# Transfers cut at partition 112, and a last stage with spread inverse roots and an affine step on GpSimd, in a two-layer graph network

## What is computed

```python
h = x @ w_in + b_in
Wij = (ssp(f_ij @ w_f1 + b_f1) @ w_f2 + b_f2) * rcut_ij[:, None]
agg = segment_sum(h[idx_j] * Wij, idx_i)
x1 = layernorm(x + ssp(agg @ w_o1 + b_o1) @ w_o2 + b_o2)

dinv = rsqrt(deg)                       # degree with the self loop
out = segment_sum((x1 @ W)[src] * (dinv[src] * dinv[dst])[:, None], dst) + b
out = relu((out - mean) * rsqrt(var + 1e-5) * gamma + beta)   # over the nodes
result = layernorm(x1 + out)                                  # over the 128 features
```

## Time and profile before

| | |
|---|---|
| runs shown | 7341.11, 7344.63, 7347.38 us, median 7344.63 us |
| the profiled execution | 7344.54 us, its span 7342.8 us |
| mean granted TensorE clock | 0.779 |
| busy share: PE, PE weight load, DVE, ACT, POOL | 79%, 56%, 72%, 48%, 69% |
| instructions | 156,129 |
| DMA | 695.39 MB, mean 95 GB/s |

### The profile page before, as it was taken

The page is one execution under the profiler, slowest core; times in us unless marked ns, Lnnn a source line. Parts: engine busy times, 40 slices in busy tenths (PEclk is TensorE's granted clock), DMA queues, the critical chain, the costliest instruction groups (busy, mean ns, idle before and its releaser), DMA issues. The chain is left out here.

```text
span 7342.8 us, 156129 instructions
## 1 busy us (share of the span) xinstructions
PE 5812.5 (79%) x41800; PEld 4127.1 (56%) x41800; DVE 5317.5 (72%) x14198; ACT 3558.1 (48%) x5657; POOL 5086.9 (69%) x5375
## 2 busy tenths in 40 slices
PE   7778787877788777777777765676999999999994
PEld 6555555555556555555555544554666666666662
DVE  7777777777778888888888873456777777777765
ACT  2555555555555555555555550063333333333334
POOL 4577777777777777777777774435777777777770
PEclk6565666666656888887777776677999999999995
DMA  4222222221223444443333327724222222222222
GB/s 129 80 85 85 86 86 72 57 57 56 57 57 99 119 118 119 122 115 98 96 98 99 97 75 234 240 95 141 77 75 77 77 76 76 76 77 76 76 77 73
DMA packets 512129, 695.39 MB, mean 95 GB/s; under 512 B 255298, under 2 KB 367644, under 8 KB 510878
## 3 DMA queue, kind: packets, MB, share of 16 engines
q1 hardware_dynamic: 317008, 347.69, 16.9%
q0 software_dynamic: 181376, 321.40, 14.9%
q10 hardware_dynamic: 13498, 24.07, 1.0%
HBM read 450.80 MB, written 241.85 MB: 94 GB/s over the span
## 5 line engine op out<-in xcount | busy, mean ns | idle before, releaser
L1694 POOL DMA_INDIRECT msg_tab<-big x3224 | 3159.3, 980 | 1065.3 <-issue 1041.2
L2245 POOL DMA_INDIRECT big<-y_parts,big x1616 | 1590.1, 984 | 551.5 <-issue 487.1
L2326 ACT CAST big<-ps 128x980 bf16<-128x980 f32 x804 | 783.9, 975 | 1277.8 <-PE ps L2274 1276.8
L2286 PE MATMUL ps<-big 128*128 128x384 bf16 x6566 | 1199.4, 326 | 0.2 <-ACT big L2326 0.2
L2378 DVE TENSOR_SCALAR big<-big,dstF 128x343 bf16<-128x343 f16 (+2 forms) x3216 | 985.3, 338 | 235.7 <-PE ps L2274 129.5
L1383 ACT CAST big<-ps 128x512 bf16<-128x512 f32 x403 | 236.0, 586 | 1511.2 <-DMA msg_tab<-big 1507.4
L2286 PEld LDWEIGHTS ps<-big 128*128 128x128 bf16 x6566 | 581.7, 97 | 350.0 <-issue 3.9
L1178 PE MATMUL ps<-big 2*128 2x512 bf16 x806 | 336.3, 509 | 547.6 <-ACT big L1367 547.4
L1186 PE MATMUL ps<-big 128*128 128x128 f32 x3224 | 706.5, 390 | 10.9 <-ACT big L1378 7.2
L1186 PEld LDWEIGHTS ps<-big 128*128 128x128 f32 x3224 | 635.4, 293 | 20.2 <-ACT big L1378 20.0
L1491 DVE TENSOR_REDUCE big<-big 128x8 f32<-128x784 f32 x403 | 629.9, 1563 | 0.0
(11 more groups left out here) (289 smaller groups left out, 10746.0 us busy)
## 6 DMA issues: line engine op xcount, KB each, us to landing
arena<-msg_tab SPq DMA_DIRECT2D x97, 727.5 KB, 4.4
big<-msg_tab SPq DMA_DIRECT2D x97, 630.5 KB
big<-in_edge_attr SPq DMA_DIRECT2D x403, 128.0 KB
msg_tab<-big POOLq DMA_INDIRECT x3224
big<-msg_tab SPq DMA_DIRECT2D x97, 388.0 KB
msg_tab<-big SPq DMA_DIRECT2D x97, 291.0 KB
big<-y_parts,big POOLq DMA_INDIRECT x1616
big<-h_parts SPq DMA_DIRECT2D x403, 48.0 KB
```

Source lines behind the costliest of these rows:

```text
L1694: nc.gpsimd.indirect_dma_start(out=m.msg_tab[:, :], out_offset=bass.IndirectOffsetOnAxis(ap=sidx[s][:, j:j + 1], axis=0), in_=row[s][:, j, ...
L2245: nc.gpsimd.indirect_dma_start(out=m.grow[s][:, 3 * D * j:3 * D * j + 3 * D], out_offset=None, in_=m.y_parts[:, :], in_offset=bass.Indirec ...
L2286: mm = pe.matmul(ps_rows, m.cnt[h][:, a, :], m.y_part[:, HALF * h + a, :], start=(h == 0 and a == 0), stop=(h == 1 and a == HALF - 1))
L2326: nc.scalar.copy(m.cnt[h][:, :, SLOTS * i:SLOTS * i + SLOTS].rearrange("p h (a w) -> p h a w", a=2), ps_cnt[i % 2][:, :, 0:SIDE * HALF].re ...
```

## The change

`node_update`: every transfer between DRAM and a tile of 125 partitions is issued as two, over partitions 0 to 111 and 112 to 124 (`PIECES`): the loads of the degrees and of `agg`, and the stores of dinv, `x1_tab`, `y_parts` and `y_tab`. The semaphores count 32 in place of 16 for a block.

`norm_and_store` is written anew. The inverse roots are read from DRAM into all 128 partitions by six transfers (`SPREAD`, of 2, 3, 5, 5, 5 and 5 blocks), before x1 on SP's queue. DVE multiplies 15 of the 25 blocks by them and POOL the other 10 (blocks 1 and 3 of each five). PE has no product there. The affine step of part C is on POOL, without the relu; the relu is folded into DVE's residual step as a maximum with 0, with the product still in PSUM. DVE's steps are interleaved so that none waits for the one just before it. There are four output buffers. The table load of ACT comes right behind the square root. The output stores and x1's loads are split at 112 partitions. All loops of the stage are written out.

```diff
+PIECES = ((0, WIDE), (WIDE, NP))
+XN = 4
+SPREAD = ((0, 2), (2, 5), (5, 10), (10, 15), (15, 20), (20, 25))
+X1_LOADS = 5
...
             def load(q, s):
-                sp.dma_start(agg[s], m.agg_sum[0:N, :].rearrange("(p c) d -> p (c d)", p=NP)[:, bass.ds(q * (B * F), B * F)]
-                             ).then_inc(tabs_in[s], 16)
+                for a, z in PIECES:
+                    sp.dma_start(agg[s][a:z, :],
+                                 m.agg_sum[0:N, :].rearrange("(p c) d -> p (c d)", p=NP)[a:z, bass.ds(q * (B * F), B * F)]
+                                 ).then_inc(tabs_in[s], 16)
...
-                    dve.wait_ge(x1_stored[s], 16 * turn + 16)
+                    dve.wait_ge(x1_stored[s], 32 * turn + 32)
...
         @block.sync
         def _(sp):
-            def load(q, s, turn):
-                sp.wait_ge(spread, free(q))
-                sp.dma_start(drow[s], m.dinv_tab[bass.ds(q * BW, BW)].rearrange("(o n) -> o n", o=1)).then_inc(row_in[s], 16)
-            over(sp, NB, load)
+            for k, (a, z) in enumerate(SPREAD):
+                sp.dma_start(dinv_bc[:, a * BW:z * BW],
+                             m.dinv_tab[a * BW:z * BW].rearrange("(o n) -> o n", o=1).to_broadcast([P, (z - a) * BW])
+                             ).then_inc(dinv_in[k], 16)
+            x1_rows = m.x1_tab.rearrange("(p c) d -> p (c d)", p=NP)
+            n = NC * D // X1_LOADS
+            for k in range(X1_LOADS):
+                for a, z in PIECES:
+                    sp.dma_start(x1[a:z, k * n:k * n + n], x1_rows[a:z, k * n:k * n + n]).then_inc(x1_in[k], 16)
...
+        @block.gpsimd
+        def _(pool):
+            for q in turns:
...
+                nc.gpsimd.tensor_tensor(part(q), part(q), scales(q), ALU.mult).then_inc(pool_scaled, 1)
+            pool.wait_ge(bn_ready, 4)
+            for q in range(NB):
+                if q > 1:
+                    pool.wait_ge(turned_back, q - 1)
+                nc.gpsimd.tensor_scalar(turned[q % 2].rearrange("f (t p) -> f t p", t=B), rows[:, q * B:q * B + B, :],
+                                        scale, shift, ALU.mult, ALU.add).then_inc(affine_done, 1)
...
+            for q in range(NB):
+                pe.wait_ge(affine_done, q + 1)
+                if q > 1:
+                    pe.wait_ge(res_done, q - 1)
                 for t in range(B):
+                    tr = pe.transpose(ps_r[q % 2][:, D * t:D * t + D], turned[q % 2][:, NP * t:NP * t + NP], m.ident[:, :])
...
+            def norm_rows(q):
+                act.wait_ge(offset_done, q + 1)
+                if q >= XN:
+                    act.wait_ge(stored[q % XN], 32 * (q // XN))
...
+            root(0)
+            for q in range(NB):
+                norm_rows(q)
+                if q + 1 < NB:
+                    root(q + 1)
...
+                nc.vector.scalar_tensor_tensor(batch, ps_r[q % 2], 0.0, batch, ALU.max, ALU.add).then_inc(res_done, 1)
...
+            def with_epsilon(q):
+                dve.wait_ge(paired, q + 1)
+                if q > 1:
+                    dve.wait_ge(normed, q - 1)
+                nc.vector.tensor_scalar(rstd[q % 2], pair[q % 2][:, :, 1], LN_EPS, None, ALU.add).then_inc(with_eps, 1)
...
+            for q in range(-1, NB + 1):
+                if q + 1 < NB:
+                    residual(q + 1)
+                if q > 0:
+                    offsets(q - 1)
+                if 0 <= q < NB:
+                    pairs(q)
+                if q + 1 < NB:
+                    measure(q + 1)
+                if 0 <= q < NB:
+                    with_epsilon(q)
```

More of the change, by code:

```diff
@@ L1833, in norm_rows @@
                                        norm.rstd[s][:, t:t + 1], ALU.subtract, ALU.mult)
[L1834 to L1849, removed]
     last.then_inc(norm.normed, 1)
@@ L2654, in norm_and_store @@
     ps, work = m.ps, m.work
-    drow = [work[0:1, 512 * s:512 * s + BW] for s in range(2)]
+    turned = [work[:, 512 * s:512 * s + BW] for s in range(2)]
     stats = work[:, 1024:1024 + 6 * NB]
@@ L2718, in _ @@
             act.wait_ge(bn_agg, 2)
             nc.scalar.activation(std, var_eps, ACT.Sqrt).then_inc(bn_std, 1)
-            act.wait_ge(bn_ready, 4)
             act.preload_act_table_set("natural_log_exp_and_others")
-            def stage(before, here, after):
-                if after:
-                    q, s, _ = after
-                    act.wait_ge(turned_back, free(q))
-                    nc.scalar.activation(turned[s].rearrange("f (t p) -> f t p", t=B), rows[:, bass.ds(q * B, B), :],
-                                         ACT.Relu, bias=shift, scale=scale).then_inc(relu_done, 1)
-                if before:
-                    q, s, turn = before
-                    act.wait_ge(stored[s], 16 * turn + 16)
-                    norm_rows_on_act(nc, act, m, norm, q, s, xn[s])
-                if here:
-                    norm_root(nc, act, norm, *here[:2])
@@ L2736, in _, with root @@
-            staged(act, NB, stage)
+            def root(q):
+                act.wait_ge(with_eps, q + 1)
+                nc.scalar.activation(rstd[q % 2], rstd[q % 2], ACT.Ln).then_inc(rooted, 1)
+                act.wait_ge(rooted, 2 * q + 1)
+                nc.scalar.activation(rstd[q % 2], rstd[q % 2], ACT.Exp, scale=-0.5).then_inc(rooted, 1)
+            def norm_rows(q):
+                act.wait_ge(offset_done, q + 1)
+                if q >= XN:
+                    act.wait_ge(stored[q % XN], 32 * (q // XN))
+                for t in range(B):
+                    last = nc.scalar.activation(xn[q % XN][:, D * t:D * t + D], x1_row(q, t), ACT.Identity,
+                                                bias=offset[q % 2][:, t:t + 1], scale=rstd[q % 2][:, t:t + 1])
+                last.then_inc(normed, 1)
@@ L2750, in _ @@
+            scale_sums(0)
+            for q in range(NB):
+                if q + 1 < NB:
+                    scale_sums(q + 1)
+                count_sums(q)
             dve.wait_ge(bn_steps, NB)
@@ L2780, in stage, with residual @@
-            def stage(before, here, after):
-                if before:
-                    norm_shift(nc, dve, norm, *before[:2])
-                if here:
-                    residual(*here)
-            staged(dve, NB, stage)
+            def residual(q):
+                for k in range(X1_LOADS):
+                    if q == -(-k * NB // X1_LOADS):
+                        dve.wait_ge(x1_in[k], 32)
+                dve.wait_ge(turned_back, q + 1)
+                batch = x1[:, q * (B * D):q * (B * D) + B * D]
+                nc.vector.scalar_tensor_tensor(batch, ps_r[q % 2], 0.0, batch, ALU.max, ALU.add).then_inc(res_done, 1)
```

173 lines of the change are left out of this document (93 added, 80 removed).

## The result

The changed kernel takes 7262.47 us (median of four runs, 7256.59 to 7265.19) against 7344.77 for the kernel before (median of four): ratio 0.9887, 95% interval 0.9871 to 0.9903, or 82 us less. The forecast was 40 us less with a range down to 7276. The direction was right, the size was not, and the time fell out of the range.

A forecast was written before the change was run, and what follows sets the result against it. Bounds: node_update's transfers on five of 16 DMA engines, part A a row's trip through DMA and PE, part C ACT. −7.7 − 36 − 1.0 + 6 − 1.2 = −39.9 from 7344.5 gives 7305 us; forecast 7296 to 7316, range 7276 to 7325.

The forecast's parts named there:

- The round is 2.2 + d + 0.2: Part C: the variance step waits for all of POOL's affine step, length d (1.25 us); round 3.65, +6 us.
- the tie: Part C: POOL starts its affine step 2.2 us into DVE's round, DVE reaches its variance step at 2.3.
- the floor of 2.5: Part C: least round, 2.5 to 2.6 us, from DVE's 2.3 per block, 2.5 with gaps.
- DVE slips ahead: Part C: tie falls DVE's way in all or half the rounds, −19 to −7; total 7280 to 7292, chance 0.22.
- Part A: Last stage's start, first roots load to aggregate: roots 4, DVE 29, POOL's exclusion 4.4, sum 37.4 instead of 73.4, −36 us.
- the roots come slowly: Part A: roots load at 128 GB/s instead of 351, part A gains only 14 us; total 7327, chance 0.08.
- node_update: Waits inside −3.5, its end −4.7, two more degree loads +0.5: together −7.7 us, between −11 and 0.
- The pieces bring nothing: Split transfers queue behind each other; node_update and tail terms fall to +0.5 and −0.7; total 7314, chance 0.05.
- Part B: Up to the first residual: table load no longer ahead of the affine step, POOL starts slightly later than ACT would, −1.0 us.
- The tail: Last residual to the end: no ACT wait for a store, and output stores on more engines, −1.2 us.
- Slower than before: Part C: POOL's affine step decides; gain gone at d = 2.9 us, measurably slower above 3.5; chance 0.03.
- The affine step is long: Part C: POOL's affine step takes 1.7 to 2.1 us, round 4.1 to 4.5; total 7316 to 7325, chance 0.16.

The follow-up runs named there:

- x1 in one load: The changed kernel with the last stage's x1 rows loaded as one load of two pieces instead of five: 7284.26 us in a single run.
- variance late: The changed kernel with one more DVE statistics instruction just ahead of the variance step in each round of part C: 7272.2 us, ratio 0.9895.
- POOL's step twice: The changed kernel with POOL doing its affine step twice per batch, first into a buffer nobody reads: 7266.38 us, ratio 0.9885.
- the split alone: The kernel before with only node_update's transfers split at 112 partitions: 7336.21 us, ratio 0.9983.
- three small edits: The changed kernel with ACT's root one batch ahead, epsilon as bias of ACT's Ln, and 12 instead of 10 part A products on POOL: 7252.38 us, ratio 0.9868.

## Why the prediction was wrong, point by point

**The failed step is part C: "The round is 2.2 + d + 0.2".** It was to give +6 and gave −29.0; 35 of the 40 us by which the sum was off are there. By the prediction's own case without a hold (2.55 a round, −20), 26 of the 35 are the hold and 9 the floor. Its inputs were good: d 1.25 against 1.237, and POOL's start 2.2 us behind the residual against 7219.21 − 7217.10 = 2.11. Three things were wrong.

First, the tie. The variance step was put at 2.3 and came at 2.12, 0.01 us behind POOL's start. What no row of before showed is that, by the start times of the trace, POOL's step has a beginning in which it excludes nobody: the one row of an exclusion had DVE 0.55 us in. Yet the tie is worth little. With the variance step moved out of it, the round was 2.22; and in the two runs where the step was held, part C was still 21 and 23 us shorter than before.

Second, what a hold costs. The sum let every round pay the whole of d. A held step waits only for the rest of POOL's, and the round after it is free; that the late residual delays POOL too is the likely reason, read from the order of the steps. With holds the rounds measured 2.43 (x1 in one load) and 2.53 (variance late), not 3.65; a round with holds is 3.29, but its neighbour is 1.78. With POOL's step done twice the sum fails by 2.4 us a round, though there DVE could pass between the two steps.

Third, the floor of 2.5. It took DVE's 2.3 of busy time, added gaps, and made DVE the bound; the bound is ACT's circle of 2.2, near the 2.1 that the prediction gave ACT. In the changed order no step waits for the one just ahead of it, and their times overlap: the residual at 7217.10 starts 0.09 behind the start of a step that lasts 0.17. From residual to residual are 7219.27 − 7217.10 = 2.17, of which DVE idles 0.32. So the rival "DVE slips ahead", with 0.22, had the outcome, a step that isn't held, but not quite the mechanism: DVE came 0.00 to 0.14 us behind POOL and not ahead of it. Its best case of 2.6 was still 0.4 above what came.

The rule cited for d, 2.9 cycles an element for a step over 8 bytes (GPSIMD Engine Reference of the Trainium skill, Performance pitfalls for Q7 kernels), gives 1.2 us by itself, and the prediction added 0.2 fixed to make 1.4. Measured were 1.237, and 1.21 from start to start in "POOL's step twice": the trace agrees with the page's figure alone, and the 0.2 was too much. On the exclusion itself the skill (SBUF — State Buffer, Who interferes with whom) says that whichever of the two instructions is issued first has the shared ports for its whole length. The held steps agree; the steps whose recorded start was up to 0.15 us behind POOL's do not. Whether POOL already has the ports at its recorded start no run shows.

**Part A: −36 forecast, −41.9 measured**, just past its far end of −41 (4 + 29 would be −40; likewise the 60 us of slow roots are −13 and not −14). Right in kind (share near 1 and DVE packed), and the roots came at 404 GB/s, so "the roots come slowly" is out. Mis-sized were the spacing, 0.585 us instead of 0.72 (−5.4), and the exclusion, at most 2.4 us instead of 4.4; the first roots took 4.6 instead of 4, and two waits for them were 1.1.

**node_update: −7.7 forecast, −10.5 measured**, inside its ends. The waits inside were worth 4.7 (3.0 net in the forecast), the end 5.8 (4.7). The 31 us of waits for the x1 store were nearly all slack, as the steps on L2140 had said. "The pieces bring nothing" is refuted by the split alone. (The case was to be 7314; its own terms give 7313.)

**Part B** was right. **The tail** was not: +0.3 for −1.2. The stores did become faster, from ACT's last row to the end 2.7 us instead of 4.35, but ACT now ends 7.3 us behind the last residual instead of 5.3, since it is a batch further behind DVE.

**"Slower than before"** needed d = 2.9 and more. Its point was set by the same sum, which no run bore out; no POOL step of that length was run, so where the point lies is open. **"The affine step is long"** is out: 1.237 us.

## What to carry to other kernels

Read the engines of a transfer off the DMA share and the count of its outer dimension before cutting it: 125 partitions cut as 112 + 13 gave a share near that of all 16 engines, and 124 + 1 gave four and a kernel slower than uncut. When two engines exclude each other, don't add the one's length to every round of the other: lay the steps on a time line, see which can start inside the other's step and what is left of that step then, and follow the delay through the next round. If the result hangs on a tie of 0.1 us, forecast both phases, and give the floor from starts and not from busy times.

## What was not expected of the hardware

- A small DVE step that starts up to 0.15 us behind POOL's affine step is not held; from 0.19 on it is, to within 0.04 us of POOL's end. So it is in all rows of part C in eight traces. The last free one of the changed kernel, at 0.14, and the first held one, at 0.19 in "three small edits":

```profile
7205.80 1.23 POOL L2722 TENSOR_SCALAR big<-arena,big 128x500 f32<-128x500 f32 x1 [0.84 <-PE ps L2732]
7205.94 0.14 DVE L2823 TENSOR_SCALAR big<-big 125x4 f32<-125x4 f32 x1
...
7200.25 1.23 POOL L2723 TENSOR_SCALAR big<-arena,big 128x500 f32<-128x500 f32 x1 [0.21 <-PE ps L2733]
7200.44 1.06 DVE L2825 SCALAR_TENSOR_TENSOR big<-big 125x4 f32<-125x4 f32 x1
```

- The same share moves different bytes: at 1.0 the roots went at 404 GB/s and the x1 rows at 227 to 251, in five loads or in one. On four and five engines the x1 rows had 104 and 128, 26 GB/s an engine; on 16 they have 15. What limits them there was not tried.
- In part A the two engines' long products exclude each other by the first start. POOL's ten took 1.679 us in the mean, against 1.157 of the earlier trace rows. One of them, at 7180.60, took 1.23; there DVE's product, 0.03 us behind, was held instead (1.73 us in place of 0.66). So the free beginning above holds for the small steps and not for a product:

```profile
7180.63 1.73 DVE L2768 TENSOR_TENSOR arena<-arena,big 128x500 f32<-128x500 f32 x1
```
